# Four heads' shifts turned in one bank, local values written by tokens, and the last stage's first load issued early

## The reference

```
q, k, v = split_heads(xn @ Wq), split_heads(xn @ Wk), split_heads(xn @ Wv)
k_c, v_c = blocks of 16 tokens of k and v @ Wck, Wcv          # 32 blocks
logits_c = where(pos >= block end, q . k_c / 4, NEG)
out_c = softmax(logits_c) @ v_c
tok = the tokens of the 4 blocks with the largest logits_c
out_s = softmax(where(tok <= pos, q . k[tok] / 4, NEG)) @ v[tok]
out_l = softmax(q . k over the last 33 tokens) @ v             # local window
out = (g0 * out_c + g1 * out_s + g2 * out_l) @ Wo              # g: gates, a softmax
```

## Time and profile before

| | |
|---|---|
| time, median of 3 runs (lowest to highest) | 1509.58 us (1504.55 to 1510.39) |
| the profiled execution: its time | 1507.87 us |
| its span (first to last instruction in the trace) | 1506.1 us |
| granted TensorE clock, mean over the span | 0.979 |
| busy in the span: PE, DVE, ACT, POOL | 94%, 79%, 62%, 61% |
| DMA | 113.74 MB, mean 76 GB/s |

### The profile page before, as it was taken

How to read it: one execution, slowest core, us unless ns; L and a number is a source line. 1 busy time by engine, 2 the same in 40 slices (tenths; PEclk the granted TensorE clock), 3 DMA queues, 4 the chain that set the end, 5 groups by cost and what they waited for, 6 DMA issues and landing times. The chain is left out here.

```text
span 1506.1 us, 43877 instructions
## 1 busy us (share of the span) xinstructions
PE 1420.1 (94%) x14960; PEld 1044.1 (69%) x14960; DVE 1187.8 (79%) x4544; ACT 928.4 (62%) x1684; POOL 919.1 (61%) x845
## 2 busy tenths in 40 slices
PE   6899679999999999999999999999999999999978
PEld 4566447777777777777777777777777777777657
DVE  5444288888888888888888888898888888888812
ACT  3766336666666666666666666666666666666641
POOL 4655356666666666666666666666666666666620
PEclk8999879999999999999999999999999999999989
DMA  6556942221111122222111122212222222222027
GB/s 186 205 183 211 274 73 53 52 51 45 47 45 47 50 51 51 51 51 50 47 46 46 47 50 49 48 48 51 51 51 51 51 51 51 65 51 53 9 95 234
DMA packets 217147, 113.74 MB, mean 76 GB/s; under 512 B 128872, under 2 KB 211224, under 8 KB 217112
## 3 DMA queue, kind: packets, MB, share of 16 engines
q1 hardware_dynamic: 216304, 112.88, 27.3%
q10 hardware_dynamic: 808, 0.42, 0.2%
HBM read 73.08 MB, written 40.16 MB: 75 GB/s over the span
## 5 line engine op out<-in xcount | busy, mean ns | idle before, releaser
L1150 POOL TENSOR_TENSOR sumxy<-xy 128x1024 f32<-128x1024 f32 x128 | 240.7, 1901 | 0.0
L1393 DVE TENSOR_REDUCE bmax<-q_bank 128x32 f32<-128x512 f32 (+3 forms) x512 | 219.9, 481 | 16.5 <-PE q_bank L1633 15.4
L1240 ACT ACTIVATE pts<-k_bank 128x512 f32<-128x512 f32 (+2 forms) x384 | 177.4, 490 | 42.0 <-PE k_bank L1668 41.2
L1494 DVE SCALAR_TENSOR_TENSOR mw<-sumxy,c,ex 128x1024 f32<-128x1024 f32 x128 | 176.0, 1394 | 1.5 <-issue 0.8
L1633 PE MATMUL q_bank<-ko,qo 96*128 96x512 bf16 (+3 forms) x512 | 142.9, 306 | 24.6 <-DVE bmax L1393 22.6
L1116 POOL TENSOR_TENSOR pad<-pad 128x1 f32<-128x1 f32 x32 | 6.2, 193 | 256.4 <-DVE top L1412 256.4
L1615 PE MATMUL f_bank<-xt,wfu 128*128 128x128 f32 x1024 | 162.3, 281 | 0.0
L1174 POOL TENSOR_TENSOR cw<-cw,mw 128x1024 f32<-128x1024 f32 x64 | 150.8, 2356 | 6.6 <-ACT mw L1264 1.6
L1615 PE MATMUL f_bank<-xt,wfg 128*128 128x128 f32 x1024 | 150.3, 279 | 0.0
L1615 PEld LDWEIGHTS f_bank<-xt,wfu 128*128 128x128 f32 x1024 | 139.4, 191 | 11.5
L1264 ACT ACTIVATE mw<-mw,erec 128x1024 f32<-128x1024 f32 x128 | 145.7, 1139 | 0.0
(11 more groups left out here) (211 smaller groups left out, 3340.1 us busy)
## 6 DMA issues: line engine op xcount, KB each, us to landing
qo<-s_qs SPq DMA_DIRECT2D x192, 64.0 KB, 2.2
ko<-s_ks SPq DMA_DIRECT2D x186, 64.0 KB, 2.2
s_qs<-parts SPq DMA_DIRECT2D x8, 768.0 KB, 4.7
s_ks<-parts SPq DMA_DIRECT2D x8, 768.0 KB, 6.3
s_v<-vo SPq DMA_DIRECT2D x8, 544.0 KB, 3.0
vv<-s_v SPq DMA_DIRECT2D x32, 136.0 KB, 2.3
vw<-s_v SPq DMA_DIRECT2D x64, 68.0 KB, 2.5
xin<-in_L_attn_x_dram SPq DMA_DIRECT2D x8, 512.0 KB, 6.9
```

The costliest lines, as they stand in the source:

```text
L1150: done("sum_done", g_.tensor_tensor(sumxy[:, h, :, :], xy[:, 0, h, 0:XK, None].broadcast_to([P, XK, KEYS]), xy[:, 1, h, None, :].broadcast ...
L1240: last = s.activation(pts[:, h, OFFS[j]:OFFS[j] + n], bank[:, 0:n], ACT.Exp)
L1393: last = v.tensor_reduce(bmax[:, i, h, 0:n], Q.bank(job)[:, o:o + n * BLK].rearrange("p (n j) -> p n j", j=BLK), AX.X, ALU.max)
L1494: done("mw_done", v.scalar_tensor_tensor(mw[:, h, :], sumxy[:, h, :, :].rearrange("p a b -> p (a b)"), c8[:, h, 7:8], ex[:, h % 2, :], ALU ...
```

## The change

- **Shifts.** The one-hot and shift rows of head h now stand in partitions 32h to 32h + 31 of `ko` and `qo`, and the six products of that head in the other three quarters. All four heads of a token tile are turned by one matmul with 128 weight columns: four matmuls per unit into one bank, job "a". ACT copies quarter h for head h: head 0 in `openings`, head 1 after `share(t, 2)`, heads 2 and 3 after parts 0 and 1 of head 0. The copy of head 3 releases the bank; the others count on `aug_done`.
- **Loads of parts.** 16 rows by 1 to 3 heads each: 16 DMAs for q, 16 for k, and 4 that write zeros (from a DRAM scratch `s_zero`) to the shift rows of `qo`, since `queries` and `window` now run over all 128 rows. Four DMAs on ACT's queue write the one-hot rows in place of a POOL copy.
- **Local values** are written by tokens: out is 32 tokens by 17 columns, so the ACT copy and the PE transposes of that branch go, and DVE reads job "vl" itself. The two row halves are written one after the other, with `mlp_down(t, 3)` between; its last down matmul waits for the first half. The calls move behind head 3.
- **expert_sum** moves ahead of `key_marks` (before: behind the third head's maxima).
- **Last stage.** yr0 is loaded in the loop of units beside ar0; PE's second transposes wait for ar1 alone, DVE's sum for yr1.
- Pairs of semaphores are merged (strike and pc_in, xy and cand, e8_in and nmax), with the same waits.

```diff
-            k_jobs = ["pcT", "co", "a0"]
+            k_jobs = ["pcT", "co", "a"]
             for h in range(HG):
-                k_jobs += [f"s{h}0", f"s{h}1", f"s{h}2"] + [f"a{h + 1}"] * (h < HG - 1) + [("pl0", "pl1", "vl", "tl")[h]]
-            k_jobs += ["vs", "ts"]
+                k_jobs += [f"s{h}0", f"s{h}1", f"s{h}2"] + [f"pl{h}"] * (h < 2)
+            k_jobs += ["vl", "vs", "ts"]
...
+            PARTS = ((0, 0), (2, 0)), ((0, 1), (0, 2)), ((1, 0), (1, 1))
+            def part_rows(to, src, which, half):
+                for i, pair in enumerate(PARTS):
+                    lots = [(3, i, i + 1)] + [(i, h0, h1) for h0, h1 in ((0, i), (i + 1, HG)) if h0 < h1]
+                    for quad, h0, h1 in lots:
+                        for n in range(2):
+                            o = 32 * quad + D * n
+                            yield to[o:o + D, half, h0:h1, :], src[pair[n][which]][:, h0:h1, :]
...
+                    pairs = [(qo[32 * h:32 * h + 32, half, h, :], s_zero) for h in range(HG)]
+                    pairs += part_rows(qo, q, 0, half)
+                    if keys:
+                        pairs += part_rows(ko, k, 1, half)
...
+                sp.wait_ge(S["st_y"].sem, 16 * (G + 1))
                 sp.dma_start(ar0[:, :, :], s_o[0].rearrange("i p c -> p i c")).then_inc(batch_in[0], 16)
+                sp.dma_start(yr0[:, :, :], s_y[0:G].rearrange("i p c -> p i c")).then_inc(batch_in[0], 16)
...
                         K.released(f"s{h}{j}", last)
-                    if h < HG - 1:
-                        head_shifts(t, h + 1)
+                        if h == 0 and j < 2:
+                            head_shifts(t, j + 2)
                     if h < 2:
                         K.wait_full(act, t, f"pl{h}")
                         K.released(f"pl{h}", s.activation(pT[:, h, :], K.bank(f"pl{h}")[:, :], ACT.Copy))
-                    elif h == 2:
-                        branch_values(t, 1)
...
-                    K.wait_full(act, t, f"a{h}")
-                    K.released(f"a{h}", s.activation(qo[SP3:P, t.half, h, :], K.bank(f"a{h}")[SP3:P, :], ACT.Copy))
+                    if h == 0:
+                        K.wait_full(act, t, "a")
+                    rows = slice(32 * h, 32 * h + 32)
+                    copy = s.activation(qo[rows, t.half, h, :], K.bank("a")[rows, :], ACT.Copy)
+                    if h < HG - 1:
+                        done("aug_done", copy)
+                    else:
+                        K.released("a", copy)
...
                     openings(t)
                     share(t, 2)
+                    head_shifts(t, 1)
                     head(t, 0)
...
+                    expert_sum(t)
+                    if n:
                         key_marks(n)
                     gate(t, 1)
                     if n:
                         for part in range(3):
                             block_max(n, 2, part)
-                    expert_sum(t)
...
-                    if part == 0:
-                        K.wait_read(pe, t, f"a{h}")
+                    if part == 0 and h < HG - 1:
+                        need(pe, "aug_done", t, h + 1)
+                    elif part == 0:
+                        K.wait_read(pe, t, "a")
...
+                    rows = slice(64 * r, 64 * r + 64)
+                    for k in range(2):
+                        for g in range(T // 32):
+                            i, q = divmod(g, 4)
+                            o = VW * (HG * i + 2 * r + k)
+                            last = mm(bank[32 * q:32 * q + 32, o:o + VW], pT[rows, k, 32 * g:32 * g + 32],
+                                      vw[rows, t.half, g, VW * k:VW * k + VW], start=True, stop=True, skip_group_check=True)
...
+                    K.wait_free(pe, t, "a")
                     for i in range(TT):
+                        last = mm(K.bank("a")[:, P * i:P * i + P], shift_s[:, i, :, :].rearrange("p h n -> p (h n)"),
+                                  identb[:, :], start=True, stop=True)
+                    K.filled("a", last)
...
                     for f in (2 * part, 2 * part + 1):
+                        if f == FT - 1:
+                            need(pe, "vl_half", t)
...
-                    head_shifts(t, 0)
+                    head_shifts(t)
...
-                            elif h == 2:
-                                local_ready(t)
-                            else:
-                                token_values(t, 1)
                             if h < 3:
                                 up_rows(t, "ugu"[h], (0, 1, 1)[h], part)
-                            else:
+                            elif part < 3:
                                 mlp_down(t, part)
-                            if (h, part) == (2, 3):
-                                local_values(t)
+                            if (h, part) == (3, 2):
+                                local_ready(t)
                             if n and part < 3:
                                 queries(n, h, part)
-                            if part == 2 and h < HG - 1:
-                                head_shifts(t, h + 1)
+                    local_values(t, 0)
+                    mlp_down(t, 3)
+                    local_values(t, 1)
...
-                sp.wait_ge(batch_in[0], 32)
-                sp.dma_start(yr[0][:, :, :], ys[0]).then_inc(batch_in[0], 16)
...
-                    pe.wait_ge(batch_in[n.index], 48 if n.index else 32)
+                    pe.wait_ge(batch_in[n.index], 32 if n.index == 1 else 48)
```

More of the change, by code:

```diff
@@ L273, in build @@
             b4 = sb("b4", [96, 2, 2, P], BF16)
+            zeros = sb("zeros", [32, T], BF16)
             bank = [ps(f"sbank{i}", [P, 512]) for i in range(4)]
@@ L311, in _ @@
                 g.memset(b1[:, :, :, :], 0.0).then_inc(cleared, 1)
+                g.memset(zeros[:, :], 0.0).then_inc(zeroed, 1)
                 for k, m in enumerate((ident, identb)):
@@ L879, in build @@
         projecting.close()
+        sb, _, _ = make(outer)
+        yr0 = sb("yr0", [P, TT, C])
         inner = ExitStack()
@@ L1031, in load_parts @@
                     q, k = row(qs, b)[g], row(ks, b)[g]
-                    pairs = [(to[D * n:D * n + D, half, :, :], src[r])
-                             for to, src, parts in ((qo, q, Q_ROWS), (ko, k, K_ROWS))[:2 if keys else 1] for n, r in enumerate(parts)]
-                    send(pairs, parts_in[half], N_PARTS if keys else N_PARTS // 2)
+                    pairs = [(qo[32 * h:32 * h + 32, half, h, :], s_zero) for h in range(HG)]
+                    pairs += part_rows(qo, q, 0, half)
+                    if keys:
+                        pairs += part_rows(ko, k, 1, half)
+                    send(pairs, parts_in[half], N_PARTS if keys else N_QUERIES)
                 def load_late(b, g, half):
@@ L1228, in _ @@
                 k_first = s_ks.rearrange("b r (g h d) t -> b g r d h t", g=G, d=D)[0][0]
-                for n, r in enumerate(K_ROWS):
-                    act.dma_start(ko[D * n:D * n + D, 0, :, :], k_first[r]).then_inc(parts_in[0], 16)
+                for h in range(HG):
+                    act.dma_start(ko[32 * h:32 * h + 32, :, h, :],
+                                  onehot[96:128, None, :].broadcast_to([32, 2, T])).then_inc(key_blocks, 16)
+                for dst, src in part_rows(ko, k_first, 1, 0):
+                    act.dma_start(dst, src).then_inc(parts_in[0], 16)
                 act.wait_ge(armed, 1)
@@ L1312, in openings, with selected_values @@
                     tanh(t, "g0", hidden(0), "th_done")
-                def branch_values(t, k):
-                    job = ("vs", "vl")[k]
-                    K.wait_full(act, t, job)
-                    K.released(job, s.activation(oT[:, k, :], K.bank(job)[:, :], ACT.Copy))
+                def selected_values(t):
+                    K.wait_full(act, t, "vs")
+                    K.released("vs", s.activation(oT[:, :], K.bank("vs")[:, :], ACT.Copy))
                 def lead(n):
@@ L1632, in queries @@
                         n = P * (i + 1)
-                        last = mm(bank[:, o:o + n], qo[0:SP3, t.half, h, P * i:P * i + P], ko[0:SP3, t.half, h, 0:n],
+                        last = mm(bank[:, o:o + n], qo[:, t.half, h, P * i:P * i + P], ko[:, t.half, h, 0:n],
                                   start=True, stop=(i > 0))
@@ L1693, in local_ready, with local_values @@
                         K.wait_read(pe, t, f"pl{k}")
-                def local_values(t):
+                def local_values(t, r):
                     bank = K.bank("vl")
-                    for g in range(T // 32):
-                        for h in range(HG):
-                            rows, k = slice(64 * (h // 2), 64 * (h // 2) + 64), h % 2
-                            last = mm(bank[32 * h:32 * h + VW, 32 * g:32 * g + 32], vw[rows, t.half, g, VW * k:VW * k + VW],
-                                      pT[rows, k, 32 * g:32 * g + 32], start=True, stop=True, skip_group_check=True)
```

(16 more changed lines are left out.)

95 lines of the change are left out of this document (44 added, 51 removed).

## The result

| | time, median (lowest to highest) | ratio to before, 95% interval |
|---|---|---|
| before | 1509.57 us (1504.55 to 1510.39) | |
| after | 1593.56 us (1593.18 to 1594.23) | 1.0564 [1.0541, 1.0587] |

The change costs 84 us, 5.6%. The prediction said slower, by 45 us to 1555, with 1538 to 1572 as that forecast's own range and 1530 to 1598 as the stated one. The profiled execution took 1593.26 us, its span is 1591.3, its mean clock 0.961 (before 0.979).

A forecast was written before the change was run, and what follows sets the result against it. PE, busy 94% of the span, was taken as the bound. 32 turns x 1.48 us = 47.4, plus 1.5 lead, less 3.5 tail, gave +45 us: 1555 us, own range 1538 to 1572, stated range 1530 to 1598.

The forecast's parts named there:

- The deciding step: At s02, PE waits 2.36 us per turn for ACT's copy of head 3 to release the bank; bounds 1.9 to 2.8.
- SP: Rival: SP's loop of 36 load issues sets the turn, 0.8 to 1.0 us longer than PE's, 1583 us; chance 0.14.
- local values at double cost: Rival: no weight load lies under a matmul in local values, 1.3 us more per turn, 1597 us; chance 0.08.
- The chain of five activations: ACT's copies of heads 1 to 3 and head 0's exps, from 810.03 to 812.62, putting s02 at 812.70 instead of 810.34.
- 2.15 - 0.33 = 1.82: PE's lateness: DVE's head 2 reductions come 2.15 us late, less the third saved shift call, 0.33 us.
- DVE makes its delay good in its 2.26 us pause: DVE's lateness is absorbed in its wait for POOL's candidates, which come some 0.6 us earlier because expert_sum moved forward.
- The clock falls: Rival: the pause halves PE's clock for 3 us of each turn, 48 us more, 1603 us; chance 0.04.
- The lead: Before the loop, 14 more DMAs on SP ahead of the first queries cost between 0 and 2.5 us, taken as 1.5.
- a tie: Ahead of the co matmuls, SP's last load (845.25) and PE (845.12) meet within 0.1 us; 0.1 added per turn.
- The tail: At the end, PE's 6.48 us wait for the first residual loads shrinks: gain between 0 and 6.5 us, taken as 3.5.
- 1.38 without SP: PE's lateness per turn at the end of the phase: 2.15 - 0.33 - 0.44 us, before the 0.1 for SP.

The follow-up runs named there:

- e1: The changed kernel with the four heads' shifts (job "a") in the bank of ring Y instead of ring K: 1500.05 us, 0.9942 of the kernel before.
- e6: e1 with DVE's up(t, 1) put ahead of unselected and best_pairs: 1472.40 us, 0.9749 of the kernel before.
- e11: e1 with DVE's unselected moved directly behind key_marks: 1492.47 us, 0.9879 of the kernel before.
- e5: e1 with expert_sum back in its old place behind the third head's maxima: 1511.58 us, 1.0015 of the kernel before.
- e9: e1 with DVE's unselected moved ahead of key_marks, behind expert_sum: 1564.77 us, 1.0355 of the kernel before.
- e4: The changed kernel with twelve unused 512-column bf16 matmuls into the Y bank just ahead of s02: 1582.06 us, 1.0478 of the kernel before.
- e8: e1 with the zeros written in 10 DMAs instead of 4, same bytes, 42 loads per turn: 1524.47 us, 1.0103 of the kernel before.
- e3: The changed kernel with head 0's up rows and queries issued on PE ahead of s02: 1568.21 us, 1.0403 of the kernel before.

## Why the prediction was right, and where its sizes were not

**The deciding step held.** "a" is released by ACT's copy of head 3 and PE's s02 waits for it: 32 times, the largest of PE's waits, 91.1 us where 75 was forecast. e1, which moves nothing but the bank, shows it to be more than the whole loss.

**The number is partly luck.** 1593.56 lies 22 us above the forecast's own range, 1538 to 1572. It is inside the stated range only because that was stretched to 1598 for two rivals, SP and local values at double cost, and neither came about. What filled the gap was a wait that the forecast had at nothing and a clock that it had at 1.00.

**The chain's size was off.** The pause is 3.0 us from start to start (s00-s02 1.92 to 4.91), forecast 2.36. The chain of five activations was costed at the 0.50 spacing of full-width ones. The trace of before had the better row: two of its own 32-row copies followed by another activation are 0.62 apart. The 0.63 too little was made good elsewhere. co-s00 is 0.24 shorter, 0.10 of it in the shift matmuls (with 128 columns they take 0.23 from start to start, 850.31 to 850.54, where one call was 0.33). The other 0.39 comes back between s02 and s30, in part because what was taken out had slowed its neighbours too: head 2's last queries stood 0.21 ahead of the next matmul before (820.09) and 0.12 after (907.92), and the up rows ahead of the local values took 0.64 before (820.63) where such rows take 0.45 (908.04). Of a turn with full clock, s30 starts 18.24 us behind co (890.25 to 908.49) where it was 17.74 with the local values' 1.31 inside. Without them PE is 1.81 late there; the forecast's terms give 2.15 - 0.33 = 1.82. That the two agree is luck: the chain was too short by 0.63, and 0.24 and 0.39 came back where nothing was forecast.

**The step that failed: "DVE makes its delay good in its 2.26 us pause".** It was to have no more price, and the candidates were to come 0.6 us earlier. Instead 0.56 us of idle stands ahead of the third down matmul, 0.73 from start to start. The changed kernel's DVE and POOL rows there (before, in the earlier trace rows, DVE stood idle until POOL's candidates):

```profile
865.91 1.68 DVE L1418 TENSOR_REDUCE bmax<-q_bank 128x32 f32<-128x512 f32 x4
867.50 1.97 DVE L1469 TENSOR_SCALAR unsel<-struck 128x512 bf16<-128x512 f32 x1
869.62 0.06 DVE L1397 MEMSET pad<- 128x1 f32 x1 [0.15 <-DVE unsel L1469]
869.62 0.61 DVE L1507 MAX8 c<-cand 128x8 f32<-128x64 f32 x4
870.14 0.67 DVE L1409 TENSOR_TENSOR hT<-hT,f_bank 128x512 f32<-128x512 f32 x1
```

```profile
866.70 0.63 POOL L1167 TENSOR_TENSOR cand<-t 128x256 f32<-128x256 f32 x1
867.28 3.94 POOL L1171 TENSOR_TENSOR sumxy<-xy 128x1024 f32<-128x1024 f32 x2
```

POOL's candidates wait for DVE's `xy`, and so DVE's delay came to POOL too: they start 18.04 us behind co, 18.10 before, and not 0.6 earlier (mean of 27 turns; in e1, without the pause, 14.97). But `unsel` is 2.65 us later, so the `sumxy` behind the candidates, which started 2.49 us behind `unsel`, now starts 0.21 ahead of it: the pause is filled by an `unsel` of 1.97 us. e6 (0.83 us per turn for putting `up` in front of it) and e11 (s32-vs the same 3.56 with `unsel` moved away) show that what stands ahead of `up` makes the wait; that an `unsel` of 0.41 in the same place would have made none is an estimate from the rows (`up` would end 1.56 earlier). e5 shows that moving the sum is a gain all the same, 0.46 us.

The Trainium skill, page "SBUF — State Buffer", section "SBUF: two separate sides", says that VectorE in a two-port mode and GpSimd take a shared port pair as an exclusive lock, held for the whole instruction by whichever starts first. The rows of e1, e9 and e11 agree: `unsel` ends 0.22 to 0.29 us behind POOL's instruction when it comes second, and takes 0.42 when it comes first. That `unsel` runs in such a mode, no row says.

**The clock.** The forecast had it at 1.00 in the loop. The rival "The clock falls", with a chance of 0.04 and a price of 48 us, came about in part: 17 turns of 29, 0.56 us each (s30 stands 18.79 us behind co in the long turns, 18.23 in the short ones), 0.3 in the mean. The clock itself costs more where it is low: from s02 to s10 (its mask matmul) PE needs 1.77 us in turns with full clock and 2.4 to 3.4 in 16 of the other 17. Most of that is hidden, since PE otherwise waits for DVE at head 1: 0.73 us ahead of 903.62 in a turn with full clock, nothing ahead of 862.35 in the slow one. e4, which fills the pause, confirms the mean with 11.5 us. The lead of the kernel before, by which the rival was argued, is no clean case: the clock was already at 0.53 in 185:194, ahead of that pause.

**The local values** cost what they did: 64 records in 0.66 us, twice, 10.3 ns each. Weight loads are busy for 0.63 of each 0.66 us, so they lie under the matmuls. Their rival (double) is out. It was the rule of the Trainium skill's page "TensorE: Matmul & The Clock Gate", Part 3, The mechanism; this trace doesn't bear it out for these shapes, 32 matmuls in a row on the same rows. What wasn't forecast is 0.2 to 0.3 us for going in and out of them twice. It is what is left of s32-vs: +1.93 = 1.31 moved, less 0.44 of transposes, plus 0.73 of wait, plus 0.3; e6, without that wait, leaves 0.2. The rows show where: the queries ahead of them take 0.20 (871.84) where 0.11 was, the down rows between them 1.06 (872.70) where 0.96 was.

**SP.** The forecast added 0.1 us per turn for a tie and gave SP as the bound a chance of 0.14. It costs nothing: issues run from 870.33 to 887.44, landed 1.7 us after issue (page, part 6), co at 890.25:

```profile
870.33 1.74 SPq L1038 DMA_DIRECT2D qo<-s_zero  x4
872.26 7.62 SPq L1038 DMA_DIRECT2D qo<-s_qs  x16
879.97 7.47 SPq L1038 DMA_DIRECT2D ko<-s_ks  x16
```

```profile
qo<-s_qs SPq DMA_DIRECT2D x320, 16.0 KB, 1.7
```

The price per issue was right: the 36 take 17.11 us, 17.2 forecast (the 16 parts of q 0.482 each to the next group, those of k 0.467, the four zeros 0.48). The landing is 0.5 shorter, and the turn was longer than forecast. e8 shows that the bound was real and near.

**The ends.** The tail came as forecast, 6.48 to 2.98 us. The lead was 2.5 us longer (co of the first turn 220.62 to 223.10), forecast 1.5, its upper bound 2.5: PE now stands 4.59 us for the parts of k (ahead of 198.78) and then again for DVE.

**The sum,** per turn, in us: forecast 1.38 without SP; +0.73 the third down matmul; +0.3 the clock; +0.2 to 0.3 the halves of the local values; 0.0 left at s30. That is 2.6 to 2.7, measured 2.70; times 32, plus 2.5, less 3.5, is 85. Rightly forecast sign, place and mechanism; missed were a second wait, on DVE and POOL, and a lower clock behind the pause in more than half of the turns.

## What to carry to other kernels

When several results share one PSUM bank and one release, look up who is next on that bank in its ring and where the last reader stands in its engine's program; e1 moved the job to an idle bank and got 6% back. When an engine is fed earlier, look at what else it will then do earlier and beside whom: here `sumxy` came to lie over a DVE instruction. Cost an activation by a row of its own width in the trace, with the spacing to its neighbours, not by its duration.

## What the runs showed of the hardware that was not expected

- A copy of 32 rows by 512 columns on ACT doesn't overlap its neighbours: starts 0.61 to 0.63 us apart for a duration of 0.59, and behind a share it starts only when the share's second record, the read of its sum, has ended (853.41, the copy at 853.43); full-width activations of 0.60 start 0.50 apart. Why wasn't tried.
- A DVE instruction of 0.41 us (512 columns, f32 to bf16) takes 1.37 to 1.97 us when it starts behind a running POOL instruction, and ends 0.22 to 0.29 us behind it; the two `sumxy` beside it take 3.94, 3.76 without it (e5). The other way round POOL's `xy` takes 0.12 more. It isn't so for every DVE instruction: `up` takes 0.67 us beside `sumxy` (870.14) and 0.69 with POOL idle (859.99).
- A pause of 2.84 us is followed by a lower clock in 17 of 29 turns (0.53 behind the one at 856.61), one of 2.1 us at s02 in e3 in four of five, one of 2.00 us at head 2 in e9 in nearly all (0.60). Which pause it follows and which not, the runs leave open.
- The idle time reported ahead of an instruction is some 0.17 us less than what it loses from start to start (2.84 and 3.0; 0.56 and 0.73).
